# One VectorE instruction over two PSUM banks in place of two over one, for masked scores and gated y

## Chip, cores and metric

The kernel runs on one core of one Trainium2 chip. The metric is the device time of the whole program in microseconds; the time before is the median of three runs.

## What is computed

A layer norm feeds two branches. The large one is a state-space recurrence with 32 heads of 64 channels and 64 state dimensions; the small one is an fp8 projection with a silu. The recurrence, cut to what matters:

```
proj = u @ in_proj_w.T                      # z, x, B, C, dt, theta, lambda
tc = cumsum(theta); B, C = rope(B), rope(C) # per head, cos and sin of tc
h  = alpha*h + gamma*(x B) + beta*(x_prev B_prev)
y  = einsum('bhpn,bhn->bhp', h, C) + x*D
y  = rms(y * silu(z)) @ out_proj_w.T
out = u + y * silu(ffn(u))
```

The input is 4 sequences of 1024 tokens with 128 features.

## The kernel before

`prepare` makes the normalised inputs, the weights and the decays. `units` does the recurrence, and takes most of the time. `finish` does the fp8 branch and the sum.

`units` walks 8 tiles of 512 tokens (index t), two to a sequence, and in each tile 8 groups of four heads (index q): 64 units. A unit treats its four heads as two pairs (p = 0, 1) of two (j or h). Every engine has its own program, written out in order by hand; semaphores tie them together. `at(per, t, k)` is the count that a semaphore has when item k of tile t is there.

What a unit does, with the names that matter here:

- VectorE makes the rotated B and C as products, `part` (L1005, eight `rotation` calls a unit, both tensor inputs in SBUF); GpSimd adds them in pairs into `rot` (L1168). The first product of the next unit is made at the head of the loop body, the second after the state update, the other six after the second pair of masked scores.
- VectorE turns the angles, `ang` (L979, reads `rnd` from ScalarE and PSUM buffer R[0]). TensorE's next use of R[0], `x_by_token` (L809), waits for it (L907).
- TensorE makes the scores of a pair in `Sp[0]` and `Sp[1]` (L843), and the exponents of one head at a time in the one buffer `Dp` (L825). ScalarE turns those into `E` (L1117). VectorE multiplies both into `M` (L1023), one head at a time. The pair p = 0 of the next unit is done at the end of the loop body, the pair p = 1 in its middle.
- TensorE sums y of two heads each in `Yp[0]` and `Yp[1]` (L929, L935, L945). VectorE multiplies it by `sz`, silu of z, into `yT` (L1082), one half at a time. ScalarE squares `yT` into `sq` (L1122), GpSimd adds the squares into `sqa` (L1199, and L1192 in the first unit of a tile), and at the end of a tile TensorE sums `sqa` over the partitions (L966) ahead of all work of the next tile.
- VectorE scales the transposed B into `bw` (L1015); TensorE's angles matmul (L804) and state matmuls (L895) wait for it. `x_by_token` of the next unit has two halves, i = 0 ahead of and i = 1 behind the exponents of the rows; VectorE scales each into `xk` and `xc` (L989).
- GpSimd makes `ce` (L1177) between the first and the second sum `rot`.

ScalarE's order behind the sines is: `E` of head 0 of the next unit, `sq` of half 0, `E` of head 1, `sq` of half 1, then the rounding `rnd` (L1101) of the unit after.

Of the kernel before, what the change touches and what calls it, by code (L numbers as in the profile page):

```python
# [20 lines left out]
F32 = mybir.dt.float32  # L21
BF16 = mybir.dt.bfloat16
FP8 = mybir.dt.float8e4
ALU = mybir.AluOpType
ACT = mybir.ActivationFunctionType
AX = mybir.AxisListType

P = 128
# [5 lines left out]
CS = 4  # L34
ST = CS * P
NS = TOK // ST
NQ = H // 4
# [6 lines left out]
MAGIC = 12582912.0  # L44
# [586 lines left out]
def units(nc, K, scratch, cum_stored):  # L631

    xn_d, tc_d, bc_d, cum_d, cumt_d = scratch
    with ExitStack() as ctx:
# [6 lines left out]
        def bank(name):  # L641
            return ctx.enter_context(nc.psum_tensor(name, [P, 512], F32))

        R = [bank("r0"), bank("r1")]
        Dp = bank("d")
        Op = bank("o")
        Sp = [bank("s0"), bank("s1")]
        Yp = [bank("y0"), bank("y1")]

        BC_LOADS = 16 * 6  # L650
        DUP = 16 * 4
        xns = sb("xns", [P, 2, ST])
        tcs = sb("tcs", [P, 2, ST])
        bcs = sb("bcs", [P, 2, 4, ST])
        rnd = sb("rnd", [P, ST])
        ang = sb("ang", [P, ST])
# [8 lines left out]
        E = sb("E", [P, 2, ST])  # L665
        M = sb("M", [P, 4, ST])
        bw = sb("bw", [P, 2, CS, P])
        hs = sb("hs", [P, CS - 1, 2, HD])
        sz = sb("sz", [P, 2, ST])
# [24 lines left out]
        def at(per, t, k):  # L694

            return t * per + max(k, 0) + 1
# [97 lines left out]
        def _(pe):  # L797
# [3 lines left out]
            def angles(t, q):  # L801

                w = K["w_th"][:, (q % NQ) * P:(q % NQ + 1) * P]
                nc.tensor.matmul(R[0][:], w, tcs[:, (t + q // NQ) % 2, :], start=True, stop=True).then_inc(u_ready, 1)  # L804

            def x_by_token(t, q, i):

# [72 lines left out]
            for t in range(NS):  # L880
                for q in range(NQ):
# [36 lines left out]
                    for p in range(2):  # L918

                        if live(t, q + 1):  # L920
                            pe.wait_ge(xk_ready, at(T2, t, 2 * q + 2 + p + 1))
                        w = K["w_zx"][:, (2 * q + p) * P:(2 * q + p + 1) * P]
                        nc.tensor.matmul(R[p][:], w, xns[:, t % 2, :], start=True, stop=True).then_inc(z_ready, 1)  # L923

                    for p in range(2):
                        pe.wait_ge(m_ready, at(T4, t, 4 * q + 2 * p + 2))
# [44 lines left out]
        def _(dve):  # L971
# [3 lines left out]
            def angles(t, q):  # L975

                dve.wait_ge(rounded, at(T1, t, q + 1))
                dve.wait_ge(sin_ready, at(T3, t, 3 * q))
                nc.vector.scalar_tensor_tensor(out=ang[:], in0=rnd[:], scalar=MAGIC, in1=R[0][:],  # L979
                                               op0=ALU.subtract, op1=ALU.subtract).then_inc(turned, 1)  # L980

            def x_scaled(t, q, tt, i):

                dve.wait_ge(x_ready, at(T2, t, 2 * q + i + 1))
                dve.wait_ge(y_ready, at(T2, t, 2 * q - 2))
                for dst, f in ((xk, "kk"), (xc, "cc")):
                    v = K[f][:, tt * (CS * H) + 2 * i * H:tt * (CS * H) + 2 * i * H + 2 * H].rearrange("p (c h) -> p c h", h=H)
                    v = v[:, :, 4 * (q % NQ):4 * (q % NQ) + 4].unsqueeze(3)
                    last = nc.vector.tensor_tensor(dst[:, q % 2, 2 * i:2 * i + 2, :].rearrange("p c (h d) -> p c h d", h=4),  # L989
                                                   R[i][:].rearrange("p (c h d) -> p c h d", c=2, h=4),  # L990
                                                   bcast(v, [P, 2, 4, HD]), ALU.mult)
                last.then_inc(xk_ready, 1)

# [14 lines left out]
            def b_decayed(t, q, tt):  # L1008

                dve.wait_ge(st_ready, at(T1, t, q))  # L1010
                for p in range(2):
                    dve.wait_ge(bt_ready, at(T2, t, 2 * q + p + 1))
                    v = K["dec"][:, tt * (CS * H):(tt + 1) * (CS * H)].rearrange("p (c h) -> p c h", h=H)
                    v = v[:, :, 4 * (q % NQ) + 2 * p:4 * (q % NQ) + 2 * p + 2].unsqueeze(3)
                    nc.vector.tensor_tensor(bw[:, p, :, :].rearrange("p c (j n) -> p c j n", j=2),  # L1015
                                            R[p][:].rearrange("p (c j n) -> p c j n", c=CS, j=2),
                                            bcast(v, [P, CS, 2, N]), ALU.mult).then_inc(bw_ready, 1)

            def scores(t, q, h):
                dve.wait_ge(e_ready, at(T4, t, 4 * q + h + 1))  # L1020
                dve.wait_ge(s_ready, at(T4, t, 4 * q + h + 1))
                dve.wait_ge(y_ready, at(T2, t, 2 * q - 1 + h // 2))
                nc.vector.tensor_tensor(M[:, h, :], Sp[h % 2][:], E[:, h % 2, :], ALU.mult).then_inc(m_ready, 1)  # L1023

            angles(0, 0)
            angles(0, 1)
# [5 lines left out]
                        rotation(0, 0, p, w, f)  # L1032
            b_decayed(0, 0, 0)
            scores(0, 0, 0)
            scores(0, 0, 1)
            for t in range(NS):
                def state(t, q, c):

                    into = 1
                    if c == 0:  # L1040
                        dve.wait_ge(y_ready, at(T2, t, 2 * q))
                        dve.wait_ge(st_ready, at(T1, t, q + 1))
                        if begins(t):
                            nc.vector.tensor_copy(hs[:, 0, :, :].rearrange("n p d -> n (p d)"), R[1][:, 0:2 * HD]).then_inc(hch, 2)
                            return
                    if c == CS - 1 and ends(t):
                        return
                    if c == CS - 2 and ends(t):
                        into = 2
                    dve.wait_ge(hch, at(T8, t, 8 * q + 2 * c))  # L1050
                    for p in range(2):
                        src = before(t, q, c, p)
                        dst = hs[:, c, p, :] if c < CS - 1 else K["carry"][:, t % 2, 2 * q + p, :]
                        nc.vector.scalar_tensor_tensor(
                            out=dst, in0=src, scalar=K["dtot"][:, (t * CS + c) * NP + 2 * q + p:(t * CS + c) * NP + 2 * q + p + 1],
                            in1=R[1][:, (2 * c + p) * 64:(2 * c + p) * 64 + 64], op0=ALU.mult, op1=ALU.add).then_inc(hch, into)

                for q in range(NQ):
                    tn = t if q < NQ - 1 else t + 1
                    if live(t, q + 1):  # L1060
                        rotation(t, q + 1, 0, 0, 0)
                    if live(t, q + 2):
                        angles(t, q + 2)
                    for c in range(CS):
                        state(t, q, c)
                    if live(t, q + 1):
                        rotation(t, q + 1, 0, 0, 1)
                        x_scaled(t, q + 1, tn, 0)
                        x_scaled(t, q + 1, tn, 1)
                    scores(t, q, 2)  # L1070
                    scores(t, q, 3)
                    if live(t, q + 1):
                        for p, w in ((1, 0), (0, 1), (1, 1)):
                            rotation(t, q + 1, p, w, 0)
                            rotation(t, q + 1, p, w, 1)

                    for p in range(2):
                        dve.wait_ge(sz_ready, at(T2, t, 2 * q + p + 1))
                        dve.wait_ge(y_ready, at(T2, t, 2 * q + p + 1))
                        dve.wait_ge(out_ready, at(T1, t, q))  # L1080
                        dve.wait_ge(sq_ready, at(T2, t, 2 * q))
                        nc.vector.tensor_tensor(yT[:, p, :], Yp[p][:], sz[:, p, :], ALU.mult).then_inc(yt_ready, 1)  # L1082
                    if live(t, q + 1):
                        b_decayed(t, q + 1, tn)
                    if q == 2:
                        dve.wait_ge(xn_loaded, (t + 1) * 16)
                        for i, op in enumerate((ALU.max, ALU.min)):
                            nc.vector.tensor_reduce(K["mags"][:, t * 2 + i:t * 2 + i + 1], xns[:, t % 2, :], AX.X, op).then_inc(mags_done, 1)
                    if live(t, q + 1):
                        scores(t, q + 1, 0)  # L1090
                        scores(t, q + 1, 1)

        @block.scalar
        def _(act):
# [3 lines left out]
            def rounding(t, q):  # L1098
                act.wait_ge(u_ready, at(T1, t, q + 1))
                act.wait_ge(sin_ready, at(T3, t, 3 * q))  # L1100
                nc.scalar.activation(rnd[:], R[0][:], ACT.Identity, bias=K["cols"][:, 1:2]).then_inc(rounded, 1)  # L1101

            def sines(t, q, first=False):
                act.wait_ge(turned, at(T1, t, q + 1))
# [25 lines left out]
            for t in range(NS):  # L1130
                for q in range(NQ):
# [8 lines left out]
                    for p in range(2):  # L1140
                        act.wait_ge(z_ready, at(T2, t, 2 * q + p + 1))
                        act.wait_ge(yt_ready, at(T2, t, 2 * q - 1 + p))
                        nc.scalar.activation(sz[:, p, :], R[p][:], ACT.Silu).then_inc(sz_ready, 1)  # L1143
                    if live(t, q + 2):
                        sines(t, q + 2)
                    if live(t, q + 1):
# [285 lines left out]
```

## Time and profile before

| | us |
|---|---|
| median of three runs | 1400.39 (1398.12 to 1400.63) |
| the profiled execution | 1400.26 |
| its span, first to last instruction | 1398.5 |
| VectorE busy | 1270.9 (91%) |
| TensorE matmuls busy | 1143.9 (82%) |
| ScalarE busy | 779.7 (56%) |
| GpSimd busy | 747.2 (53%) |

All times are of one profiled execution. In the lists in order of time, a row gives the start, the duration, the engine, the source line, the operation, what it writes and reads and how many instructions are merged in the row; brackets at its end give the time that the engine stood idle before it and what ended that. Successive instructions of VectorE or ScalarE overlap a little, so that the distance of two starts is less than a duration. PE is TensorE's matmul side, DVE is VectorE, ACT is ScalarE and POOL is GpSimd.

### The profile page before, as it was taken

Reading aid. Unit: us, or ns where it says so; the run is one execution under the profiler, and the core shown is the slowest. Engines: PE = TensorE matmul, PEld = TensorE weight load, DVE = VectorE, ACT = ScalarE, POOL = GpSimd, SP = SyncE. Lnnn points to the kernel's source line nnn. Section 1 sums busy time; section 2 is a strip of 40 time slices with the busy share of each in tenths; the row PEclk is TensorE's granted clock in tenths of the full one; section 3 lists DMA queues with packets and bytes.
Section 4 is the critical chain, followed back from the end, with each engine's and each line's share of the span. In section 5 each row is a group of like instructions: output and inputs, shape, how many; then the busy total and the mean of one; then the engine's idle time right before and its main releaser. Section 6 shows DMA issues by size and latency. Waiting matters only on the chain. (4 is left out here: it accounts for less than half of the span.)

```text
span 1398.5 us, 30923 instructions
## 1 busy us (share of the span) xinstructions
PE 1143.9 (82%) x11508; PEld 840.5 (60%) x11508; DVE 1270.9 (91%) x1998; ACT 779.7 (56%) x1184; POOL 747.2 (53%) x563
## 2 busy tenths in 40 slices
PE   3466269998999999999999899999998999899810
PEld 2355146666666666666667666766676666667610
DVE  5887479998999899999999999989998999899778
ACT  2222136665666666666666666666666666666431
POOL 3410035665666656655666566656665666566523
PEclk9665579999999999999999999999999999999965
DMA  7121324222422242224222423233333322222123
GB/s 171 39 83 60 94 61 108 63 63 66 108 63 63 65 108 63 63 65 108 62 63 66 96 70 67 65 80 77 66 69 73 75 63 65 62 63 63 32 87 94
DMA packets 66673, 103.83 MB, mean 74 GB/s; under 512 B 14003, under 2 KB 30876, under 8 KB 66204
## 3 DMA queue, kind: packets, MB, share of 16 engines
q1 hardware_dynamic: 66524, 101.85, 31.1%
q8 instruction: 93, 1.52, 0.5%
q14 instruction: 56, 0.46, 0.1%
HBM read 24.73 MB, written 9.96 MB: 25 GB/s over the span
## 5 line engine op out<-in xcount | busy, mean ns | idle before, releaser
L1168 POOL TENSOR_TENSOR rot<-part 128x512 f32<-128x512 f32 x256 | 382.5, 1494 | 540.7 <-DVE part L1005 489.0
L1005 DVE SCALAR_TENSOR_TENSOR part<-bcs,k_prmT,trig 128x512 f32<-128x512 f32 x512 | 501.1, 1029 | 0.9 <-DMA trig<-tri 0.9
L1117 ACT ACTIVATE E<-d 128x512 f32<-128x512 f32 x256 | 151.7, 592 | 184.2 <-PE d L825 181.9
L843 PE MATMUL s<-rot 64*128 64x128 f32 x2048 | 149.7, 285 | 23.7 <-POOL rot L1168 19.2
L1023 DVE TENSOR_TENSOR M<-s,E 128x512 f32<-128x512 f32 x256 | 163.5, 678 | 2.4 <-PE s L843 1.8
L843 PEld LDWEIGHTS s<-rot 64*128 64x128 f32 x2048 | 126.9, 188 | 62.1 <-issue 54.7
L1177 POOL TENSOR_TENSOR ce<-rot,eb 128x512 f32<-128x512 f32 x128 | 160.0, 1271 | 3.0 <-ACT eb L1139 3.0
L1199 POOL TENSOR_TENSOR sqa<-sqa,sq 128x512 f32<-128x512 f32 x112 | 142.6, 1273 | 14.2 <-ACT sq L1122 6.2
L935 PE MATMUL y<-M,xk 128*64 128x128 f32 x2048 | 140.1, 279 | 0.0
L857 PEld LDWEIGHTS o<-k_w_o,yT 128*128 128x128 f32 x1024 | 132.5, 191 | 10.4 <-DVE yT L1082 5.0
L857 PE MATMUL o<-k_w_o,yT 128*128 128x128 f32 x1024 | 134.5, 275 | 2.6 <-DVE yT L1082 2.6
L809 PE MATMUL r<-k_w_zx,xns 128*128 128x256 f32 x512 | 133.5, 383 | 3.3 <-DVE ang L979 3.3
L923 PE MATMUL r<-xns,k_w_zx 128*128 128x512 f32 x256 | 122.6, 596 | 4.2 <-DVE xc L989 4.2
L935 PEld LDWEIGHTS y<-M,xk 128*64 128x64 f32 x2048 | 109.2, 136 | 21.4 <-issue 21.4
L804 PE MATMUL r<-tcs,k_w_th 128*128 128x512 f32 x128 | 74.2, 662 | 55.8 <-DVE bw L1015 42.3
L1139 ACT ACTIVATE eb<-d 128x512 f32<-128x512 f32 x128 | 76.4, 597 | 68.4 <-PE d L832 68.4
L1143 ACT ACTIVATE sz<-r 128x512 f32<-128x512 f32 x128 | 76.4, 597 | 61.1 <-PE r L923 60.9
L989 DVE TENSOR_TENSOR xk<-r,k_kk 128x512 f32<-128x512 f32 x128 | 88.0, 688 | 23.1 <-PE r L809 22.5
L1122 ACT ACTIVATE sq<-yT 128x512 f32<-128x512 f32 x128 | 80.0, 625 | 49.0 <-DVE yT L1082 49.0
L809 PEld LDWEIGHTS r<-k_w_zx,xns 128*128 128x128 f32 x512 | 96.9, 192 | 15.9 <-issue 4.8
L825 PE MATMUL d<-k_cum,k_pick 111*128 111x512 bf16 x256 | 99.6, 389 | 0.0
L1082 DVE TENSOR_TENSOR yT<-y,sz 128x512 f32<-128x512 f32 x128 | 81.7, 677 | 7.7 <-PE y L945 7.7
(242 smaller groups left out, 1827.8 us busy)
## 6 DMA issues: line engine op xcount, KB each, us to landing
trig<-tri SPq DMA_DIRECT2D x512, 128.0 KB, 2.4
bcs<-bc_t SPq DMA_DIRECT2D x16, 256.0 KB, 4.1
bcs<-bc_t SPq DMA_DIRECT2D x32, 128.0 KB, 4.1
a_big<-in_L_attn_u SPq DMA_DIRECT2D x4, 512.0 KB, 6.2
xn_t<-a_xnT SPq DMA_DIRECT2D x1, 2048.0 KB, 7.6
tc_t<-a_tcT SPq DMA_DIRECT2D x1, 2048.0 KB, 12.4
bc_t<-a_tmp SPq DMA_DIRECT2D x1, 2048.0 KB, 7.4
tcs<-tc_t SPq DMA_DIRECT2D x8, 256.0 KB, 3.0
```

Of the source, the lines that this page charges most:

```text
L809: last = nc.tensor.matmul(R[i][:, 256 * c:256 * c + 256], xns[:, (t + q // NQ) % 2, (2 * i + c) * P:(2 * i + c + 1) * P], K["w_zx"][:, DI ...
L825: nc.tensor.matmul(Dp[:], K["pick"][:, head * P:head * P + P], K["cum"][0:D_ROWS, q % 2, h, :], start=True, stop=True).then_inc(d_ready, 1)
L843: last = nc.tensor.matmul(Sp[j][:, k], rot[rows, q % 2, p, 0, k], rot[rows, q % 2, p, 1, k], start=True, stop=True)
L857: last = nc.tensor.matmul(Op[:, k], yT[:, p, k], K["w_o"][:, (2 * q + p) * P:(2 * q + p + 1) * P], start=False, stop=q == NQ - 1 and c == ...
L923: nc.tensor.matmul(R[p][:], w, xns[:, t % 2, :], start=True, stop=True).then_inc(z_ready, 1)
L935: nc.tensor.matmul(Yp[p][m:m + 64, k], xk[:, par, c, 128 * p + m:128 * p + m + 64], M[:, 2 * p + j, k], start=False, stop=c == 0 and begin ...
L1005: nc.vector.scalar_tensor_tensor(out=part[:, 2 * p + f, :], in0=bcs[:, (t + q // NQ) % 2, 2 * w + f, :], scalar=col, in1=trig[:, p, 1 - f, ...
L1023: nc.vector.tensor_tensor(M[:, h, :], Sp[h % 2][:], E[:, h % 2, :], ALU.mult).then_inc(m_ready, 1)
L1117: nc.scalar.activation(E[:, h % 2, :], Dp[:], ACT.Exp).then_inc(e_ready, 1)
L1168: nc.gpsimd.tensor_tensor(rot[:, q % 2, p, w, :], part[:, 2 * p, :], part[:, 2 * p + 1, :], ALU.add).then_inc(rot_ready, 1)
L1177: nc.gpsimd.tensor_tensor(ce[:, p, :], rot[:, q % 2, p, 1, :], eb[:, p, :], ALU.mult).then_inc(ce_ready, 1)
L1199: nc.gpsimd.tensor_tensor(sqa[:], sqa[:], sq[:, p, :], ALU.add).then_inc(sqa_ready, 1)
```

## The change

The two R buffers, the two score buffers and the two y buffers become three tensors of two PSUM banks each, `R`, `S_both` and `Y_both`, with views of one bank for TensorE. The two instructions of 512 columns that make `M` of a pair become one of 1024, and so do the two that make `yT`. Each raises its semaphore by 2 at its end, and waits for what both halves need. The order on every engine is otherwise kept. The uses of R only change their notation.

```diff
-        R = [bank("r0"), bank("r1")]
+        def banks(name):
+            t = ctx.enter_context(nc.psum_tensor(name, [P, 2, 512], F32))
+            return t, [t[:, 0, :], t[:, 1, :]]
+
+        _, R = banks("r")
         Dp = bank("d")
         Op = bank("o")
-        Sp = [bank("s0"), bank("s1")]
-        Yp = [bank("y0"), bank("y1")]
+        S_both, Sp = banks("s")
+        Y_both, Yp = banks("y")
...
-            def scores(t, q, h):
-                dve.wait_ge(e_ready, at(T4, t, 4 * q + h + 1))
-                dve.wait_ge(s_ready, at(T4, t, 4 * q + h + 1))
-                dve.wait_ge(y_ready, at(T2, t, 2 * q - 1 + h // 2))
-                nc.vector.tensor_tensor(M[:, h, :], Sp[h % 2][:], E[:, h % 2, :], ALU.mult).then_inc(m_ready, 1)
+            def scores(t, q, p):
+                dve.wait_ge(e_ready, at(T4, t, 4 * q + 2 * p + 2))
+                dve.wait_ge(s_ready, at(T4, t, 4 * q + 2 * p + 2))
+                dve.wait_ge(y_ready, at(T2, t, 2 * q - 1 + p))
+                nc.vector.tensor_tensor(M[:, 2 * p:2 * p + 2, :], S_both[:], E[:], ALU.mult).then_inc(m_ready, 2)
...
-                    scores(t, q, 2)
-                    scores(t, q, 3)
+                    scores(t, q, 1)
...
-                    for p in range(2):
-                        dve.wait_ge(sz_ready, at(T2, t, 2 * q + p + 1))
-                        dve.wait_ge(y_ready, at(T2, t, 2 * q + p + 1))
-                        dve.wait_ge(out_ready, at(T1, t, q))
-                        dve.wait_ge(sq_ready, at(T2, t, 2 * q))
-                        nc.vector.tensor_tensor(yT[:, p, :], Yp[p][:], sz[:, p, :], ALU.mult).then_inc(yt_ready, 1)
+                    dve.wait_ge(sz_ready, at(T2, t, 2 * q + 2))
+                    dve.wait_ge(y_ready, at(T2, t, 2 * q + 2))
+                    dve.wait_ge(out_ready, at(T1, t, q))
+                    dve.wait_ge(sq_ready, at(T2, t, 2 * q))
+                    nc.vector.tensor_tensor(yT[:], Y_both[:], sz[:], ALU.mult).then_inc(yt_ready, 2)
...
                     if live(t, q + 1):
                         scores(t, q + 1, 0)
-                        scores(t, q + 1, 1)
```

## Rows read from the trace of the kernel before

**Rows 1.** Stretches: us and instructions of PE, PEld, DVE, ACT, POOL; granted clock; DMA.
```profile
450.00:750.00 300.00, 277.44 (x2928) 202.40 (x2927) 287.62 (x467) 190.86 (x291) 182.36 (x133) 1.00 0.33 73
```
**Rows 2.** VectorE in order of time, one unit of the last tile of a sequence.
```profile
709.18 1.28 DVE L1082 TENSOR_TENSOR yT<-y,sz 128x512 f32<-128x512 f32 x2
...
711.58 1.27 DVE L1023 TENSOR_TENSOR M<-s,E 128x512 f32<-128x512 f32 x2
712.77 1.07 DVE L1005 SCALAR_TENSOR_TENSOR part<-bcs,k_prmT,trig 128x512 f32<-128x512 f32 x1
713.77 0.68 DVE L979 SCALAR_TENSOR_TENSOR ang<-rnd,r 128x512 f32<-128x512 f32 x1
...
717.96 0.69 DVE L989 TENSOR_TENSOR xk<-r,k_kk 128x512 f32<-128x512 f32 x1 [0.19 <-PE r L809]
...
719.17 1.28 DVE L1023 TENSOR_TENSOR M<-s,E 128x512 f32<-128x512 f32 x2
720.36 6.09 DVE L1005 SCALAR_TENSOR_TENSOR part<-bcs,k_prmT,trig 128x512 f32<-128x512 f32 x6
726.38 1.28 DVE L1082 TENSOR_TENSOR yT<-y,sz 128x512 f32<-128x512 f32 x2
```
**Rows 3.** TensorE in order of time in the same unit.
```profile
711.11 1.12 PE L804 MATMUL r<-tcs,k_w_th 128*128 128x512 f32 x2 [0.78 <-DVE bw L1015]
...
714.66 1.03 PE L809 MATMUL r<-k_w_zx,xns 128*128 128x256 f32 x4
```
**Rows 4.** Groups by line and shape: busy us, mean ns; a sum of 1024 columns.
```profile
L501 DVE TENSOR_TENSOR a_s<-a_dl,a_rowb 128x1024 f32<-128x1024 f32 x1 | 1.2, 1226 | 0.2 <-DVE a_st L494 0.2
```
**Rows 5.** ScalarE in order of time in the unit of rows 2.
```profile
709.89 0.63 ACT L1122 ACTIVATE sq<-yT 128x512 f32<-128x512 f32 x1 [0.58 <-DVE yT L1082]
710.43 0.58 ACT L1117 ACTIVATE E<-d 128x512 f32<-128x512 f32 x1
710.91 0.62 ACT L1122 ACTIVATE sq<-yT 128x512 f32<-128x512 f32 x1
```
**Rows 6.** GpSimd in order of time in the unit of rows 2, one instruction a row.
```profile
709.34 1.27 POOL L1168 TENSOR_TENSOR rot<-part 128x512 f32<-128x512 f32 x1 [0.63 <-DVE part L1005]
710.60 1.27 POOL L1199 TENSOR_TENSOR sqa<-sqa,sq 128x512 f32<-128x512 f32 x1
712.02 1.28 POOL L1199 TENSOR_TENSOR sqa<-sqa,sq 128x512 f32<-128x512 f32 x1
...
717.88 2.50 POOL L1177 TENSOR_TENSOR ce<-rot,eb 128x512 f32<-128x512 f32 x2
```
**Rows 7.** All engines just ahead: a product of VectorE and a sum of GpSimd.
```profile
706.99 1.71 POOL L1168 TENSOR_TENSOR rot<-part 128x512 f32<-128x512 f32 x1 [0.63 <-DVE part L1005]
707.50 1.76 DVE L1005 SCALAR_TENSOR_TENSOR part<-bcs,k_prmT,trig 128x512 f32<-128x512 f32 x1
```
**Rows 8.** VectorE in the third unit of a tile, behind the two reductions `mags`.
```profile
678.77 0.74 DVE L1005 SCALAR_TENSOR_TENSOR part<-bcs,k_prmT,trig 128x512 f32<-128x512 f32 x1
679.43 0.68 DVE L979 SCALAR_TENSOR_TENSOR ang<-rnd,r 128x512 f32<-128x512 f32 x1
```
**Rows 9.** A unit of the first tile of a sequence: VectorE and TensorE.
```profile
584.01 1.28 DVE L1082 TENSOR_TENSOR yT<-y,sz 128x512 f32<-128x512 f32 x2
...
589.78 1.03 PE L809 MATMUL r<-k_w_zx,xns 128*128 128x256 f32 x4
...
593.09 0.69 DVE L989 TENSOR_TENSOR xk<-r,k_kk 128x512 f32<-128x512 f32 x1 [0.23 <-PE r L809]
```
**Rows 10.** The first unit of a tile: GpSimd's one addition, and VectorE's next wait.
```profile
641.67 1.28 POOL L1192 TENSOR_TENSOR sqa<-sq 128x512 f32<-128x512 f32 x1 [0.99 <-ACT sq L1122]
...
648.21 0.69 DVE L989 TENSOR_TENSOR xk<-r,k_kk 128x512 f32<-128x512 f32 x1 [0.70 <-PE r L809]
```
**Rows 11.** The end of a tile: TensorE's sum over the squares, and VectorE.
```profile
623.09 1.05 PE L966 MATMUL d<-k_ones,sqa 128*128 128x1 f32 x8 [0.78 <-POOL sqa L1199]
...
625.87 0.69 DVE L979 SCALAR_TENSOR_TENSOR ang<-rnd,r 128x512 f32<-128x512 f32 x1 [2.19 <-ACT rnd L1101]
```

More of the change, by code:

```diff
@@ L803, in angles @@
                 w = K["w_th"][:, (q % NQ) * P:(q % NQ + 1) * P]
-                nc.tensor.matmul(R[0][:], w, tcs[:, (t + q // NQ) % 2, :], start=True, stop=True).then_inc(u_ready, 1)
+                nc.tensor.matmul(R[0], w, tcs[:, (t + q // NQ) % 2, :], start=True, stop=True).then_inc(u_ready, 1)
             def x_by_token(t, q, i):
@@ L922, in _ @@
                         w = K["w_zx"][:, (2 * q + p) * P:(2 * q + p + 1) * P]
-                        nc.tensor.matmul(R[p][:], w, xns[:, t % 2, :], start=True, stop=True).then_inc(z_ready, 1)
+                        nc.tensor.matmul(R[p], w, xns[:, t % 2, :], start=True, stop=True).then_inc(z_ready, 1)
                     for p in range(2):
@@ L978, in angles @@
                 dve.wait_ge(sin_ready, at(T3, t, 3 * q))
-                nc.vector.scalar_tensor_tensor(out=ang[:], in0=rnd[:], scalar=MAGIC, in1=R[0][:],
+                nc.vector.scalar_tensor_tensor(out=ang[:], in0=rnd[:], scalar=MAGIC, in1=R[0],
                                                op0=ALU.subtract, op1=ALU.subtract).then_inc(turned, 1)
@@ L989, in x_scaled @@
                     last = nc.vector.tensor_tensor(dst[:, q % 2, 2 * i:2 * i + 2, :].rearrange("p c (h d) -> p c h d", h=4),
-                                                   R[i][:].rearrange("p (c h d) -> p c h d", c=2, h=4),
+                                                   R[i].rearrange("p (c h d) -> p c h d", c=2, h=4),
                                                    bcast(v, [P, 2, 4, HD]), ALU.mult)
@@ L1015, in b_decayed @@
                     nc.vector.tensor_tensor(bw[:, p, :, :].rearrange("p c (j n) -> p c j n", j=2),
-                                            R[p][:].rearrange("p (c j n) -> p c j n", c=CS, j=2),
+                                            R[p].rearrange("p (c j n) -> p c j n", c=CS, j=2),
                                             bcast(v, [P, CS, 2, N]), ALU.mult).then_inc(bw_ready, 1)
-            def scores(t, q, h):
-                dve.wait_ge(e_ready, at(T4, t, 4 * q + h + 1))
-                dve.wait_ge(s_ready, at(T4, t, 4 * q + h + 1))
-                dve.wait_ge(y_ready, at(T2, t, 2 * q - 1 + h // 2))
-                nc.vector.tensor_tensor(M[:, h, :], Sp[h % 2][:], E[:, h % 2, :], ALU.mult).then_inc(m_ready, 1)
+            def scores(t, q, p):
[3 more added lines that the diff above has]
+                nc.vector.tensor_tensor(M[:, 2 * p:2 * p + 2, :], S_both[:], E[:], ALU.mult).then_inc(m_ready, 2)
             angles(0, 0)
@@ L1034, in _ @@
             scores(0, 0, 0)
-            scores(0, 0, 1)
             for t in range(NS):
@@ L1100, in rounding @@
                 act.wait_ge(sin_ready, at(T3, t, 3 * q))
-                nc.scalar.activation(rnd[:], R[0][:], ACT.Identity, bias=K["cols"][:, 1:2]).then_inc(rounded, 1)
+                nc.scalar.activation(rnd[:], R[0], ACT.Identity, bias=K["cols"][:, 1:2]).then_inc(rounded, 1)
             def sines(t, q, first=False):
@@ L1142, in _ @@
                         act.wait_ge(yt_ready, at(T2, t, 2 * q - 1 + p))
-                        nc.scalar.activation(sz[:, p, :], R[p][:], ACT.Silu).then_inc(sz_ready, 1)
+                        nc.scalar.activation(sz[:, p, :], R[p], ACT.Silu).then_inc(sz_ready, 1)
                     if live(t, q + 2):
```

## Prediction, made blind

> **What bounds the kernel now.** I read the busy time by stretches first, then the engines in order of time over one unit, then the two odd units of a tile. In the middle of the span VectorE is busy 287.6 of 300 us and TensorE 277.4 [rows 1], so either may set the end. A common unit lasts 17.20 us, from `yT` at 709.18 to `yT` at 726.38 [rows 2]; there are 64 units, eight to each of 8 tiles. I call the start of `yT` T and count from there. VectorE is idle only once in the unit, 0.19 us ahead of the second `xk`, at T+8.78 [rows 2], waiting for TensorE's second `x_by_token`. TensorE in its turn stood idle 0.78 us for `bw` before it began the chain that leads there [rows 3]. So two strands run side by side from `yT` to the second `xk`. One is VectorE's own order. The other is TensorE: from `bw` through its angles matmul and the first `x_by_token` at T+5.48 to `xk`, 3.30 us later [rows 3, 2]. VectorE's strand is only 0.19 us the shorter. From `xk` to the next `yT`, 8.42 us, VectorE never waits [rows 2]. Two narrow places tie the strands. The first `x_by_token` waits for `ang`, which ends at 714.45, and starts at 714.66 [rows 2, 3]. And VectorE's products and GpSimd's sums can't run at once: a product ahead of `yT` took 1.76 us while GpSimd's sum ran, and ended 0.56 us behind it [rows 7]; one with no sum beside it takes 0.74 [rows 8].
>
> **What the merge saves.** Two instructions of 512 columns take 1.19 us of VectorE's order (711.58 to 712.77) and 1.28 from start to end [rows 2]. No row has 1024 columns from PSUM; the nearest, from SBUF, takes 1.226 [rows 4]. An instruction's successor starts 0.08 ahead of its end (two starts are 0.60 apart where one takes 0.68 [rows 2, 8]), which gives 1.14. The reads from PSUM may be a hair quicker than those from SBUF. I take 1.21 from start to end and 1.13 in order, a saving of 0.06 for each merge, with 0 and 0.08 as ends (nothing saved; the whole overlap saved). Three merges a unit make 0.18 us, 64 units 11.5 us, if every one lay on the path.
>
> The Trainium skill ("VectorE: DVE Perf Modes", the section on the TRN2 errata) says that the latency is exposed between instructions, so that one large tile pays it once, and its table gives 120 cycles of 0.96 GHz for an instruction that reads PSUM. By it each merge would save an estimated 0.125 us and 192 merges 24 us; the starts 0.60 us apart in rows 2 leave less than 0.08, and I go by them.
>
> **What the merge delays.** The half 0 of `yT` is done 0.68 us after T now, and the square of it starts at T+0.71, the exponential `E` of head 1 at T+1.25, the second square at T+1.73 [rows 5]. Merged, `yT` ends at T+1.21, whatever half is asked for. The three move to T+1.24, T+1.78 and T+2.26: 0.53 us later, as ScalarE does them in that order. `M` of the next unit's pair 0 now needs both heads' `E`. That ends at T+2.36 and lets `M` start at T+2.40. VectorE would be there at T+1.13+1.19=T+2.32, so a wait of 0.08 takes the place of the saving, and the product behind `M` starts at T+3.53, against T+3.59 now [rows 2].
>
> GpSimd adds the two squares. Now it comes free from `rot` at T+1.43, finds the first square ready, and its two additions run T+1.42 to T+2.69 and T+2.84 to T+4.12 [rows 6]. VectorE's product, started at T+3.59, is held by the second one: 1.07 instead of 0.74, ending 0.54 behind GpSimd [rows 2, 6]. With the first square ending at T+1.87 and 0.07 to GpSimd (its sum at 709.34 began 0.08 behind the product's end at 709.26 [rows 6, 7]), the additions run from T+1.94 and, 1.42 later, from T+3.36 to T+4.64. The product at T+3.53 comes 0.17 behind the second addition's start, so it is held to the end: it ends at T+5.18, and `ang` starts at T+5.11 instead of T+4.59: 0.52 us later.
>
> **Where that lands.** `ang` ends at T+5.79; with 0.06 to TensorE, taken between the 0.03 of `yT` to its square [rows 2, 5] and that 0.08, the first `x_by_token` starts at T+5.85 instead of T+5.48. The second `xk` follows 3.30 later at T+9.15, with up to 0.08 more for weights that can't be loaded ahead. VectorE's own strand gets there at T+8.59+0.52=T+9.11. Both agree: `xk` at about T+9.17, 0.39 late. Behind it the merged `M` of pair 1 gives 0.06 back. In the first tile of a sequence TensorE's `x_by_token` starts at T+5.77 anyway [rows 9], and `xk` at T+9.08, where VectorE was idle 0.23. There VectorE's own strand is the later one, T+8.85+0.52, 0.29 late. GpSimd's `ce`, which ends at T+11.20 just as the six products begin at T+11.18 [rows 6, 2], moves by 0.52 with the products ahead of it and holds the first of the six by up to 0.1 more. So such a unit costs +0.33 in either kind of tile (0.39-0.06; 0.29-0.06+0.1). I bound it by 0.2 (no hold by `ce`) and 0.45.
>
> Not every unit is such. Per tile:
> - Five common units (the second, and the fourth to the seventh): +0.33 each. The last tile has four with all of this, so 39.
> - The first: GpSimd makes one addition, behind both squares, [rows 10], so it too runs late and holds the product, about 0.45 us. But VectorE waits 0.70 for TensorE there [rows 10], which covers it, and TensorE's strand gains what `yT` and `M` of pair 1 save: -0.12. Were that cover gone it would be +0.3.
> - The third: two reductions of 1.2 us stand ahead of `M`, so that the product starts at T+4.7, behind the additions; it isn't held now (0.74 [rows 8]) and won't be. All three savings count: -0.19.
> - The end of a tile, 7 times: TensorE waits 0.78 for the sum of the squares, and VectorE then 2.19 for the rounding behind it [rows 11]. The sum is ready 0.52 later: +0.52-0.06, +0.46.
>
> Edits with one answer: the wait of `yT` for its second half costs nothing, since both halves of y are complete before VectorE gets there (it isn't idle ahead of `yT` [rows 2]); nor does `M` of pair 1, behind a unit of other work; ScalarE's next exponentials wait for the whole `M`, which now ends at T+3.61, ahead of the old pair's end at T+3.67. No instruction is moved past a DMA queue. The new notation of R does nothing.
>
> The sum: 39 x 0.33 = 12.9; 7 x 0.46 = 3.2; 8 x -0.12 = -1.0; 8 x -0.19 = -1.5. Together +13.6. The profiled execution is 1400.26 us, 1.8 beyond its span, and the median of the runs is 1400.39, so that one stands for the other: 1400.4+13.6 = **1414 us**.
>
> **The rivals.** Within 0.2% (2.8 us) is about what a measurement of this kernel can tell from no change.
> - *Plain saving, faster.* The late squares find room: VectorE's product isn't held longer, or both strands have slack that the rows hide. Then 56 units give 0.12 (one of three savings lies beside TensorE's strand and is eaten by the wait for `E`), 8 give 0.19, and the ends of tiles take 3.6 back: 1400.4-6.7-1.5+3.6 = 1396, or 1392 without the last. For it speaks that VectorE is 96% busy [rows 1], against it the product already held today [rows 2, 6]. 13%.
> - *The order flips, same.* The product gets in ahead of the second addition, a matter of 0.17 us. Then the product takes 0.74, VectorE has 0.4 in hand, and a unit gains 0.12; but at the end of a tile the additions are later by another 0.9, 7 times. 1400.4-8.2+3.6+6.3 = 1402. Against it: both starts hang on the same square, so that a slow `yT` moves them together. 8%, and 4% more for an effect of some 0.05 a unit.
> - *It doesn't do what it says, slower.* An instruction over two banks takes as long as two: then `yT` and `M` of pair 1 save nothing and the delays stand: 64 x 0.12 = 8 more, 1422. 7%, from there upward.
>
> The Trainium skill ("SBUF — State Buffer", "Who interferes with whom") bears on the second: a VectorE instruction with two SBUF inputs and a GpSimd one that reads SBUF exclude each other for the whole instruction, and the order of issue decides who blocks. The trace agrees (1.76 and 1.07 against 0.74), and by that rule a shift of 0.17 us would turn the result to 1402.
>
> **How the numbers follow.** Slower has my forecast, 68%, and the third rival, 7%: 75%. Same 12%, faster 13%. The forecast's own range: 39 units at 0.2 give 1409, the bound of nothing saved 1422. The range for all is 1396 to 1422: it takes in the plain saving's nearer end.
>
> **What would show it.** Right: `yT` and `M` once each at about 1.21 us; the square of half 0 at T+1.24; a wait of VectorE for `E` ahead of the first `M`; GpSimd's additions at T+1.94 and T+3.36; the product behind `M` at some 1.65 us instead of 1.07; TensorE waiting for `ang` ahead of `x_by_token`; common units of 17.5 us. Wrong: a product of 0.74 there, the additions still at T+1.42, or merged instructions of 1.28 us.

## The result, and the profile after

The changed kernel takes 1425.66 us (median of 6 runs, 1423.24 to 1426.62) where the kernel before takes 1398.14 (6 runs, 1395.67 to 1400.63). The ratio is 1.0195, 95% interval 1.0179 to 1.0211. The forecast was 1414, with a range of 1396 to 1422: the sign was right, the size was half of what came, and the time lies outside the range. The span of the profiled execution went from 1398.5 to 1423.7 us. The sum was made against 1400.4, and the later runs put the kernel before at 1398.1, so that the loss is 25 to 27.5 us where 13.6 was forecast.

The unit that answers to [rows 2], VectorE in order of time:

```profile
718.25 1.21 DVE L1083 TENSOR_TENSOR yT<-y,sz 128x1024 f32<-128x1024 f32 x1
...
720.70 1.23 DVE L1027 TENSOR_TENSOR M<-s,E 128x1024 f32<-128x1024 f32 x1
721.85 1.60 DVE L1009 SCALAR_TENSOR_TENSOR part<-bcs,k_prmT,trig 128x512 f32<-128x512 f32 x1
723.36 0.68 DVE L983 SCALAR_TENSOR_TENSOR ang<-rnd,r 128x512 f32<-128x512 f32 x1
...
727.50 0.69 DVE L993 TENSOR_TENSOR xk<-r,k_kk 128x512 f32<-128x512 f32 x1
...
728.71 1.21 DVE L1027 TENSOR_TENSOR M<-s,E 128x1024 f32<-128x1024 f32 x1
729.84 6.09 DVE L1009 SCALAR_TENSOR_TENSOR part<-bcs,k_prmT,trig 128x512 f32<-128x512 f32 x6
735.85 1.21 DVE L1083 TENSOR_TENSOR yT<-y,sz 128x1024 f32<-128x1024 f32 x1
```

ScalarE, GpSimd and TensorE in the same unit, for [rows 5], [rows 6] and [rows 3]:

```profile
719.50 0.63 ACT L1122 ACTIVATE sq<-yT 128x512 f32<-128x512 f32 x1 [1.05 <-DVE yT L1083]
720.04 0.58 ACT L1117 ACTIVATE E<-d 128x512 f32<-128x512 f32 x1
...
720.21 2.68 POOL L1199 TENSOR_TENSOR sqa<-sqa,sq 128x512 f32<-128x512 f32 x2 [0.53 <-ACT sq L1122]
...
724.09 1.13 PE L813 MATMUL r<-k_w_zx,xns 128*128 128x256 f32 x4 [0.27 <-DVE ang L983]
```

Each merge does what it says: one instruction of 1.21 us for a pair of 1.28. But `yT` now gives its first half away only at its end. The first square starts at T+1.25 instead of T+0.71. GpSimd, free before, waits 0.53 us for it, a wait that [rows 6] do not have. The additions run until T+4.64, the product behind `M` sits behind them and takes 1.60 us instead of 1.07, and `ang` starts at T+5.11. TensorE waits for `ang`, and the unit lasts 17.60 us instead of 17.20.

The end of a tile is where the forecast missed. TensorE there, at two tile ends of the changed kernel; in both the state matmuls L899 are 32:

```profile
483.22 1.05 PE L970 MATMUL d<-k_ones,sqa 128*128 128x1 f32 x8 [1.38 <-POOL sqa L1199]
484.13 1.10 PE L808 MATMUL r<-tcs,k_w_th 128*128 128x512 f32 x2
485.17 1.69 PE L899 MATMUL r<-xk,bw 128*64 128x64 f32 x32
486.79 0.61 PE L829 MATMUL d<-k_cum,k_pick 111*128 111x512 bf16 x1
487.33 1.93 PE L847 MATMUL s<-rot 64*128 64x128 f32 x16
```

```profile
775.82 1.05 PE L970 MATMUL d<-k_ones,sqa 128*128 128x1 f32 x8 [1.38 <-POOL sqa L1199]
776.74 1.10 PE L808 MATMUL r<-tcs,k_w_th 128*128 128x512 f32 x2
777.77 1.15 PE L899 MATMUL r<-xk,bw 128*64 128x64 f32 x32
778.85 0.39 PE L829 MATMUL d<-k_cum,k_pick 111*128 111x512 bf16 x1
779.17 1.16 PE L847 MATMUL s<-rot 64*128 64x128 f32 x16
```

Both had the same wait, 1.38 us where the kernel before had 0.78 [rows 11]. After the first, the state matmuls take 1.69 us for 1.15 and the scores 1.93 for 1.16. The stretches show why. The columns are those of [rows 1]; the clock is the first number behind the five engines. Of the changed kernel, at a tile end of the kind of [rows 11]:

```profile
630.00:632.00 2.00, 1.73 (x10) 1.19 (x10) 0.76 (x1) 0.16 (x1) 0.21 (x1) 1.00 0.32 73
632.00:634.00 2.00, 2.00 (x26) 1.40 (x25) 0.89 (x3) 0.69 (x1) 0.00 (x0) 0.58 0.00 0
634.00:636.00 2.00, 2.00 (x18) 1.71 (x17) 1.86 (x7) 0.60 (x1) 0.00 (x0) 0.56 0.00 0
636.00:638.00 2.00, 1.47 (x8) 0.87 (x6) 0.73 (x3) 1.09 (x2) 1.26 (x1) 1.00 0.00 0
```

The same place in the kernel before:

```profile
625.00:627.00 2.00, 2.00 (x40) 1.67 (x41) 1.10 (x4) 1.28 (x2) 0.00 (x0) 1.00 0.00 0
```

TensorE's granted clock falls from its level of 2.4 GHz to that of 1.2 for some 3.4 us, and TensorE works through all of it. In the kernel before it stays at the upper level through every tile end.

To see where the 25 us lie I took the start of each `yT` from both traces and compared unit by unit. The start of the first `yT` differs by up to 7 us between the executions of these kernels, and is left out. The table gives the sum over each kind of unit, against the kernel before, in us. "Last two" are the two distances between the last three `yT`. Each row is one profiled execution; for late_add, e_first and combo2 it was the quickest one, 3.9, 4.7 and 3.0 us under the median of their runs.

| kernel | common (38) | first of a tile (8) | third (8) | tile end (7) | last two | sum |
|---|---|---|---|---|---|---|
| forecast | +12.9 (39) | -1.0 | -1.5 | +3.2 | 0 | +13.6 |
| changed | +14.4 | -0.5 | -1.3 | +10.9 | +1.7 | +25.2 |
| m_only | -2.6 | -0.4 | -0.8 | -0.4 | -0.1 | -4.2 |
| yt_only | +16.0 | 0.0 | -0.6 | +14.2 | +0.2 | +29.8 |
| fill | +14.3 | -0.5 | -1.3 | +3.3 | +0.2 | +15.9 |
| late_add | +15.8 | -0.3 | -1.4 | +4.7 | +0.3 | +19.2 |
| late_add2 | +0.4 | -1.0 | +2.1 | +4.8 | +1.5 | +7.7 |
| end_split | +14.4 | -0.5 | -1.3 | -0.5 | +1.6 | +13.7 |
| e_first | -4.1 | -0.7 | +0.6 | +15.2 | 0.0 | +10.9 |
| combo2 | -0.2 | -1.0 | +2.1 | -0.4 | +0.2 | +0.7 |
| best | -3.2 | -0.3 | -1.3 | -0.4 | -0.2 | -5.5 |

Of the changed kernel's seven tile ends two cost 0.47 us each, and five 1.97 to 2.01.

### The profile page after: what moved, and what is told of

It reads as the page before. It is cut to its first block and busy times, and to the rows that moved or that the text cites. A ratio compares the mean times of both kernels' runs of the same rounds, so it can differ in the third digit from the quotient of the medians.

```text
span 1423.7 us, 30603 instructions
## 1 busy us (share of the span) xinstructions
PE 1163.9 (82%) x11508; PEld 850.5 (60%) x11508; DVE 1292.1 (91%) x1806; ACT 779.6 (55%) x1184; POOL 747.6 (53%) x563
## 5 line engine op out<-in xcount | busy, mean ns | idle before, releaser
L1009 DVE SCALAR_TENSOR_TENSOR part<-bcs,k_prmT,trig 128x512 f32<-128x512 f32 x512 | 530.8, 1087 | 1.5 <-DMA trig<-tri 1.4
L847 PE MATMUL s<-rot 64*128 64x128 f32 x2048 | 153.3, 290 | 23.4 <-POOL rot L1168 16.5
L847 PEld LDWEIGHTS s<-rot 64*128 64x128 f32 x2048 | 130.6, 193 | 63.0 <-issue 56.1
L1027 DVE TENSOR_TENSOR M<-s,E 128x1024 f32<-128x1024 f32 x128 | 156.0, 1219 | 7.1 <-ACT E L1117 4.4
L813 PE MATMUL r<-k_w_zx,xns 128*128 128x256 f32 x512 | 137.6, 391 | 9.1 <-DVE ang L983 8.1
L813 PEld LDWEIGHTS r<-k_w_zx,xns 128*128 128x128 f32 x512 | 93.8, 191 | 32.3 <-DVE ang L983 13.9
L899 PEld LDWEIGHTS r<-xk,bw 128*64 128x64 f32 x1792 | 60.6, 144 | 51.7 <-DVE bw L1019 44.3
```

The lines of the kernel that those rows point to most:

```text
L813: last = nc.tensor.matmul(R[i][:, 256 * c:256 * c + 256], xns[:, (t + q // NQ) % 2, (2 * i + c) * P:(2 * i + c + 1) * P], K["w_zx"][:, DI ...
L847: last = nc.tensor.matmul(Sp[j][:, k], rot[rows, q % 2, p, 0, k], rot[rows, q % 2, p, 1, k], start=True, stop=True)
L1009: nc.vector.scalar_tensor_tensor(out=part[:, 2 * p + f, :], in0=bcs[:, (t + q // NQ) % 2, 2 * w + f, :], scalar=col, in1=trig[:, p, 1 - f, ...
L1027: nc.vector.tensor_tensor(M[:, 2 * p:2 * p + 2, :], S_both[:], E[:], ALU.mult).then_inc(m_ready, 2)
```

## The experiments

### Which merge costs: M alone, and yT alone

The first kernel takes `yT` apart again, the second `M`:

```diff
# m_only, against the changed kernel
-  nc.vector.tensor_tensor(yT[:], Y_both[:], sz[:], ALU.mult).then_inc(yt_ready, 2)
+  for p in range(2):
+      ...
+      nc.vector.tensor_tensor(yT[:, p, :], Yp[p], sz[:, p, :], ALU.mult).then_inc(yt_ready, 1)
# yt_only, against the changed kernel
-  nc.vector.tensor_tensor(M[:, 2 * p:2 * p + 2, :], S_both[:], E[:], ALU.mult).then_inc(m_ready, 2)
+  for h in (2 * p, 2 * p + 1):
+      ...
+      nc.vector.tensor_tensor(M[:, h, :], Sp[h % 2], E[:, h % 2, :], ALU.mult).then_inc(m_ready, 1)
```

> The changed kernel with yT in two instructions again, M still merged. Theory A (the loss comes from yT alone: its first half is squared 0.53 us late, GpSimd's additions of squares follow, and hold VectorE's product behind M): the first square starts 0.71 us after yT, the additions at 1.42, ang 4.55 to 4.6 us after yT, a common unit lasts 17.14 (17.20 less one saved 0.06), no half-speed stretch at the end of a tile; the time is 3 to 5 us under the kernel before, 1393 to 1396. Rival B (the joint wait of M for both heads' exponentials costs): M waits for E, common units stay at 17.4 or more, time 1405 or more. Rival C (an instruction over two banks costs more than its length): M keeps its part of the loss, two of the three merges, 1410 or more.

Measured: 1392.59 us, ratio 0.9957 (0.9941 to 0.9973). VectorE in a common unit of m_only:

```profile
702.32 1.27 DVE L1084 TENSOR_TENSOR yT<-y,sz 128x512 f32<-128x512 f32 x2
...
704.72 1.21 DVE L1027 TENSOR_TENSOR M<-s,E 128x1024 f32<-128x1024 f32 x1
705.85 1.13 DVE L1009 SCALAR_TENSOR_TENSOR part<-bcs,k_prmT,trig 128x512 f32<-128x512 f32 x1
706.90 0.67 DVE L983 SCALAR_TENSOR_TENSOR ang<-rnd,r 128x512 f32<-128x512 f32 x1
```

`M` starts at T+2.40 as before, with no wait for the second head, and `ang` at T+4.58. A common unit lasts 17.14, 0.06 less. Rivals B and C fall, and the loss is that of `yT`, as theory A has it; that it goes through GpSimd's additions is tested further down. The time came out 6.6 us under the kernel before where 3 to 5 were expected; the trace has 4.2.

> The changed kernel with M in two instructions again, yT still merged. Theory A: the additions start 1.95 us after yT, the product behind M is held until they end, ang starts at 5.11, common units last 17.65 (17.60 and one saving of 0.06 less), the end of a tile costs about 2 us in some tiles with TensorE at half its clock; time 1426 to 1430. Rival B (the wait of M for both heads): without it the units fall back to 17.2 to 17.3, time 1400 to 1406. Rival C: one of three merges left, 1405 to 1410.

Measured: 1428.15 us, ratio 1.0206 (1.0188 to 1.0225). VectorE in a common unit:

```profile
702.19 1.21 DVE L1084 TENSOR_TENSOR yT<-y,sz 128x1024 f32<-128x1024 f32 x1
...
704.52 1.27 DVE L1028 TENSOR_TENSOR M<-s,E 128x512 f32<-128x512 f32 x2
705.72 1.66 DVE L1009 SCALAR_TENSOR_TENSOR part<-bcs,k_prmT,trig 128x512 f32<-128x512 f32 x1
707.30 0.67 DVE L983 SCALAR_TENSOR_TENSOR ang<-rnd,r 128x512 f32<-128x512 f32 x1
```

The product takes 1.66 us and `ang` starts at T+5.11, though `M` of the first head starts without a wait. All seven tile ends are followed by half clock here. The whole loss is that of `yT`. In the traces the merged `M` takes 2.8 us off it in the common, first and third units; the measured times of the changed kernel and of this one can't be told apart.

### Is it the clock at the tile ends?

Five matmuls of zeros, which serve nothing, fill TensorE's wait at a tile end:

```diff
-                pe.wait_ge(sqa_ready, at(T2, t, T2))
                 pe.wait_ge(e_ready, at(T4, t, T4 + 2 if live(t, NQ) else T4))
+                for i in range(5):
+                    nc.tensor.matmul(Dp[:], K["zeros_bf"][0:MASK_ROWS, :], K["cum"][0:MASK_ROWS, 0, 0, :], start=True, stop=True)
+                pe.wait_ge(sqa_ready, at(T2, t, T2))
```

> The changed kernel with five matmuls of 512 columns of zeros at the end of each tile, between the projection and the sum over the squares, where TensorE otherwise waits. Nothing else is changed. Theory D (in five of seven tile ends the longer wait of TensorE is followed by 3.4 us at half clock, which costs 1.5 us each): the granted clock stays 1.0 through all the tile ends, each end costs 0.5 us over the kernel before instead of 2.0, time 1417 to 1419 against 1425.7 for the changed kernel. Rival (the 1.5 us come from another chain, such as the late rounding or a DMA): no change, 1425 to 1427.

Measured: 1414.76 us, ratio 1.0115 (1.0095 to 1.0135), 11 us under the changed kernel. TensorE at a tile end:

```profile
624.10 1.24 PE L969 MATMUL d<-k_cum,k_zeros_bf 85*128 85x512 bf16 x5
625.64 1.05 PE L972 MATMUL d<-k_ones,sqa 128*128 128x1 f32 x8 [0.30 <-POOL sqa L1201]
...
627.59 0.92 PE L899 MATMUL r<-xk,bw 128*64 128x64 f32 x24
```

The additions are as late as in the changed kernel, but the wait is 0.30 us, the clock stays at its upper level from the first unit to the last, and all seven ends cost 0.47 on average; the forecast had 0.46 without any half clock. So added work made the kernel faster: 7.6 us at the tile ends (10.9 against 3.3), and 1.5 in the last two units, where the changed kernel had one such stretch. What is left of the 11 us is no more than the executions scatter ahead of the first unit. The expected 1417 to 1419 had left out the stretch in the last two units.

The next kernel takes away the cause of the long wait instead, by taking `yT` apart in the last unit of a tile alone:

```diff
+  if q < NQ - 1:
       nc.vector.tensor_tensor(yT[:], Y_both[:], sz[:], ALU.mult).then_inc(yt_ready, 2)
+  else:
+      for p in range(2):
+          ...
+          nc.vector.tensor_tensor(yT[:, p, :], Yp[p], sz[:, p, :], ALU.mult).then_inc(yt_ready, 1)
```

> The changed kernel with yT in two instructions in the last unit of each tile alone, 7 of its 63 crossings. Theory D (at a tile end the late first square delays the additions, so TensorE waits 1.37 us instead of 0.78, and that wait is what is followed by the half clock): TensorE waits 0.8 us for the additions there, no half clock, the ends cost nothing over the kernel before instead of 10.9 us in all; the common units keep 0.38 us each; 1411 to 1415. Rival (the half clock comes from the slower common units ahead of it): half-speed stretches stay, 1418 or more.

Measured: 1409.52 us, ratio 1.0084 (1.0069 to 1.0098). TensorE at a tile end:

```profile
625.15 1.05 PE L970 MATMUL d<-k_ones,sqa 128*128 128x1 f32 x8 [0.78 <-POOL sqa L1207]
...
627.10 0.92 PE L899 MATMUL r<-xk,bw 128*64 128x64 f32 x24
```

The wait is 0.78 us as before the change, no tile end is followed by half clock, and the ends cost -0.5 us in all. The slower common units ahead of them don't matter for it. The time is below the 1411 to 1415 expected, although one stretch of half clock, 1.5 us dear, is left between the last two `yT`.

### Is it GpSimd's hold on the product?

The squares stay late; only GpSimd's additions are to let the product go first. In a first try the wait named a product that had been made long before, so that it held nothing:

```diff
+  if q < NQ - 1:                        # late_add
+      pool.wait_ge(part_ready, at(T8, t, 8 * (q + 1) + 1))
+  if q < NQ - 1 and live(t, q + 2):     # late_add2, in its place
+      pool.wait_ge(part_ready, at(T8, t, 8 * (q + 2) + 1))
```

> The changed kernel, except that in all units but the last of a tile GpSimd's additions of squares wait for VectorE's product behind M. The squares are as late as before. Theory A (what costs is that the second addition holds this product): the product takes 0.74 us, ang starts 4.25 us after yT, TensorE's strand sets the second xk at 8.75, common units last 17.05 to 17.15; only the tile ends keep their loss of 7 times 0.5 to 2.0 us; time 1400 to 1406, or near 1395 if the clock holds too. Rival E (the late exponential of head 1 or the late squares cost by another way, not through GpSimd): common units stay at 17.5 to 17.6, time 1422 to 1426.

Measured: 1417.89 us, ratio 1.0135 (1.0115 to 1.0155). The additions ran as early as in the changed kernel, 0.05 us later for the wait itself, so this says nothing on theory A. It is of use in another way: common units cost 0.04 more than in the changed kernel, yet only one tile end of seven was followed by half clock, with the same waits there. Its tile ends cost 4.7 us in all instead of 10.9, 6.2 us less, and its trace is 6.0 us under that of the changed kernel. It is one execution of a kernel whose five took 1414.03 to 1421.88 us, so the count at the tile ends may differ from one execution to the next.

> The changed kernel, except that in all units but the last of a tile GpSimd's additions of squares wait for VectorE's product behind M (the wait of late_add named a product that was long done). The squares are as late as in the changed kernel. Theory A (what costs in a common unit is that the second addition holds this product): the product takes 0.74 us, ang starts 4.25 us after yT, common units last 17.05 to 17.15 (17.60 changed, 17.20 before); the tile ends keep 0.5 to 2.0 us; 1395 to 1406. Rival E (the late squares and the late exponential of head 1 cost by another way): common units stay at 17.5 to 17.6, time 1415 to 1426.

Measured: 1405.27 us, ratio 1.0057 (1.0040 to 1.0074). VectorE and then GpSimd in a common unit:

```profile
711.07 1.21 DVE L1083 TENSOR_TENSOR yT<-y,sz 128x1024 f32<-128x1024 f32 x1
...
714.66 0.74 DVE L1009 SCALAR_TENSOR_TENSOR part<-bcs,k_prmT,trig 128x512 f32<-128x512 f32 x1
715.32 0.68 DVE L983 SCALAR_TENSOR_TENSOR ang<-rnd,r 128x512 f32<-128x512 f32 x1
...
717.38 1.34 DVE L1009 SCALAR_TENSOR_TENSOR part<-bcs,k_prmT,trig 128x512 f32<-128x512 f32 x1
...
722.17 6.26 DVE L1009 SCALAR_TENSOR_TENSOR part<-bcs,k_prmT,trig 128x512 f32<-128x512 f32 x6
```

```profile
715.48 2.69 POOL L1201 TENSOR_TENSOR sqa<-sqa,sq 128x512 f32<-128x512 f32 x2 [2.98 <-DVE part L1009]
...
720.03 2.50 POOL L1177 TENSOR_TENSOR ce<-rot,eb 128x512 f32<-128x512 f32 x2
```

The product takes 0.74 and `ang` starts at T+4.25, both to the hundredth as expected. The 0.38 us of the common units are gone (0.01 on average). They don't fall to the 17.1 that I had expected, because the additions now hold VectorE's next product, 1.34 us instead of 0.74. The rotated sum and `ce`, which wait for that product, come later too: `ce` ends 0.36 us behind the start of the six products, which take 6.26 instead of 6.09. Theory A holds for the cause, and my working missed what the moved additions collide with; in the third unit, which had no collision, they cost 0.26. One tile end of seven is followed by half clock, as in late_add, and one such stretch lies in the last two.

> The changed kernel with ScalarE's order turned round: the exponential of head 1 ahead of the first square. M then doesn't wait, and both squares come later still (first addition 2.4 us after yT, second after 3.8). Theory A with GpSimd and VectorE excluding each other by order of issue: the product behind M waits for the first addition's end only (3.7), gets in ahead of the second, takes 0.7 to 0.9 us; common units 17.05 to 17.2; the tile ends are worse, 1.1 us later than before or more, and at half clock after it; 1396 to 1410. Rival (later squares always cost more): common units above 17.6, time above 1426.

The edit puts `decays(t, q + 1, 1)` ahead of `squares(t, q, 0)` in ScalarE's program. Measured: 1413.46 us, ratio 1.0117 (1.0100 to 1.0135). VectorE in a common unit, then GpSimd in the next:

```profile
692.80 1.21 DVE L1083 TENSOR_TENSOR yT<-y,sz 128x1024 f32<-128x1024 f32 x1
...
695.13 1.21 DVE L1027 TENSOR_TENSOR M<-s,E 128x1024 f32<-128x1024 f32 x1
696.26 0.76 DVE L1009 SCALAR_TENSOR_TENSOR part<-bcs,k_prmT,trig 128x512 f32<-128x512 f32 x1
...
701.51 0.69 DVE L993 TENSOR_TENSOR xk<-r,k_kk 128x512 f32<-128x512 f32 x1 [0.57 <-PE r L813]
```

```profile
712.25 2.96 POOL L1198 TENSOR_TENSOR sqa<-sqa,sq 128x512 f32<-128x512 f32 x2 [0.96 <-ACT sq L1122]
```

This is the rival of the flipped order, made to happen. The product gets in ahead of the second addition, takes 0.76, and GpSimd's pair takes 2.96 instead of 2.69: now the second addition is the one that takes longer, behind the product. Squares that are later still make the common units faster (-0.11), and the tile ends dearer (2.2 us each, five of them with half clock). Which of the two engines is held follows from which is first. The time lies above the 1410 expected, since the tile ends were that dear.

### A better version

> The changed kernel with yT split in the last unit of each tile and GpSimd's additions in the others waiting for the product behind M: what I would build from theories A and D. Common units 17.05 to 17.15, tile ends as before, no half clock; 1388 to 1393, against 1392.6 for M alone merged.

Measured: 1398.40 us, ratio 1.0004 (0.9994 to 1.0014): no gain. The expected 1388 to 1393 left out the collision that late_add2 shows.

The last kernel takes each kind of unit's best: `M` merged; `yT` merged but in the last unit of a tile; and ScalarE's order by unit:

```diff
+  early = q not in (2, NQ - 1)
-  squares(t, q, 0)
-  if live(t, q + 1):
+  if early and live(t, q + 1):
       decays(t, q + 1, 1)
+  squares(t, q, 0)
+  if not early and live(t, q + 1):
+      decays(t, q + 1, 1)
   squares(t, q, 1)
```

> Built on what the runs before showed: M merged everywhere, yT merged in all units but the last of each tile; ScalarE makes the exponential of head 1 ahead of the squares, except in the third unit (where VectorE's product comes late anyway) and the last. Each kind of unit is then to take its best value so far against the kernel before: common -0.11, first -0.09, third -0.16, tile end -0.06, no half clock: 38, 8, 8 and 7 of them, together -6.7 us, 1391 to 1392 where the kernel before has 1398. Rival: the late additions of one kind of unit spoil the next kind, which these averages don't show: 1394 or more.

> M alone merged, the same kernel as m_only, for a comparison on the same chip: 4.2 us under the kernel before by its trace, 1394.

Measured, on one chip: 1394.18 us, ratio 0.9960 (0.9946 to 0.9975), and for `M` alone 1393.57, ratio 0.9963 (0.9951 to 0.9975). Both beat the kernel before by 0.4%, and can't be told apart. By the traces the elaborate one gains 5.5 us and the plain one 4.2. The elaborate one missed its 1391 to 1392, and its rival is what happened: most of its common units gain 0.13, but two lost 0.8. In both, as in one unit of e_first, VectorE's product waited for the DMA that writes its input `trig`. VectorE and GpSimd in one of them, whose `yT` starts at 565.11:

```profile
569.18 1.55 DVE L1009 SCALAR_TENSOR_TENSOR part<-bcs,k_prmT,trig 128x512 f32<-128x512 f32 x1 [0.54 <-DMA trig<-tri]
```

```profile
567.49 2.69 POOL L1210 TENSOR_TENSOR sqa<-sqa,sq 128x512 f32<-128x512 f32 x2 [0.96 <-ACT sq L1130]
```

The product comes 0.54 us late, finds the second addition running and is held to its end, which is later here than in the changed kernel. The order that the early exponential gives is kept only while the product starts on time. The plain kernel, `M` alone, is what I would keep.

## Where the prediction held and where it failed

Point by point, by its own steps, for the common unit of the last tile of a sequence. The two rightmost columns count from the start of `yT`, but for durations.

| step | forecast | measured |
|---|---|---|
| merged instruction, start to end | 1.21 | 1.21 |
| first square starts | 1.24 | 1.25 |
| `M` starts | 2.40 | 2.45 |
| product starts | 3.53 | 3.60 |
| additions run | 1.94 to 4.64 | 1.96 to 4.64 |
| `ang` starts | 5.11 | 5.11 |
| first `x_by_token` starts | 5.85 | 5.84 |
| second `xk` starts | 9.17 | 9.25 |
| unit, in all | 17.53 | 17.60 |

- *The mechanism* was the one forecast: m_only and yt_only show that the loss is that of `yT`, late_add2 that it goes through GpSimd's additions. A common unit was put at +0.33 and cost +0.38. In the second tile of a sequence the strand from `x_by_token` to `xk` took 3.41 us where I had used 3.30 and left "up to 0.08" for weights that can't be loaded ahead: I took the lower part of it. In the first tile `xk` came 0.28 us late, as forecast, but `ce` held the first of the six products for 0.18 us where I had taken up to 0.1. Together that is 1.6 us of the miss.
- *The first unit of a tile* was put at -0.12. In the first tile of a sequence it gained 0.13, in the second nothing, which no row of mine had told apart. Sum: 0.5 us. *The third*, at -0.19, gained 0.17.
- *The tile end* is the step that failed. I put 0.46 on each, 3.2 us in all, and seven cost 10.9. Without half clock the measured value is what I had (0.47 in fill and in two ends of the changed kernel). But TensorE's wait grew from 0.78 to 1.38 us, and I priced the work behind it at the durations of the kernel before. In five of seven ends that work ran at half clock and cost 1.5 us more: 7.7 us of the miss of 11.6. One more such stretch in the last two units adds 1.5. I had looked at how long each engine works and who waits for whom, and not at what a longer idle stretch does to the clock of the work that follows. The kernel before has half clock only ahead of its first unit and behind the `yT` of its last, so its tile ends gave no warning; but the forecast named no bound for it, and the range was too narrow by that. Without the half clock (7.6 us at the tile ends, 1.5 in the last two units) the terms as measured sum to 16.1, and 1400.4+16.1 = 1416.5 lies within the range.
- *The rivals.* The wait of `M` for both heads, counted at 0.08 us, was 0.12 (M at 2.45, 2.33 without it), and lay beside the hold. That an instruction over two banks costs two did not happen. The flip of the order was 0.23 us away (the product at T+3.60, the second addition at T+3.37) where I had reckoned 0.17, and e_first made it happen; its tile ends were dearer than I had reckoned because of the clock.

Still open is what decides at which place a wait is followed by half clock. Two tile ends of seven escaped with the same wait of 1.38 us, in late_add and late_add2 six of seven. And TensorE waits as long at two more places, in the last two units, where it stands idle for `bw`. In the kernel before it does so too, with nothing behind it; in the changed kernel, in end_split and in late_add2 one of the two waits is followed by half clock at once. The second of these places, in the kernel before and in the changed one:

```profile
1316.19 0.92 PE L895 MATMUL r<-xk,bw 128*64 128x64 f32 x24 [1.46 <-DVE bw L1015]
```

```profile
1338.96 1.55 PE L899 MATMUL r<-xk,bw 128*64 128x64 f32 x24 [1.40 <-DVE bw L1019]
```

So the length of the one wait does not decide alone. The traces show that shortening or filling the wait at the tile ends ended the half clock there, not where its limit lies.

## What to carry to other kernels

An instruction over twice the data gives its first half away only at its end. What it saves is small where two instructions overlap already, 0.06 us here; so ask who starts on the first half, and follow that engine until something can't move. Here it was a square, an addition, and an exclusive hold on the engine that the merge was to relieve. And when a change makes TensorE wait longer, price the work behind the wait at half clock as well, as one end of the range.

## What the runs showed of the hardware

- A VectorE instruction of 1024 columns over two neighbouring PSUM banks took 1.211 us for `yT` and 1.219 for `M` as means, against 0.677 and 0.678 for one bank. No price for crossing the bank shows: 1024 columns from SBUF took 1.226 [rows 4].
- A wait of TensorE longer by 0.6 us (1.38 for 0.78) was followed by about 3.4 us at half clock in five of seven places, beginning 1.2 to 2.4 us behind the wait, with TensorE busy in between and throughout. With five matmuls of zeros inside the wait it came in none. With the same wait, yt_only had it at all seven tile ends, and late_add and late_add2 at one each, in one profiled execution of each. Two waits of 1.46 us in the kernel before were not followed by it.
- VectorE's product takes 0.74 us alone. Where GpSimd's addition was running first, it ended 0.55 us behind the addition (median of 55 in the changed kernel, at most 0.74). Where the product got in between, in e_first, it took 0.76, and the second addition 1.54 for 1.27.
